# Rotation spread over the expert slots, keys stored once and doubled by their loads

## The chip, the cores and the metric

One core of a Trainium2 chip runs the whole kernel. The metric is the device time in microseconds of one launch, the median of several. The core's engines are TensorE (PE), VectorE (DVE), ScalarE (ACT) and GpSimd (POOL); SyncE (SP) only issues DMAs. DMAs issued by SyncE, ScalarE and GpSimd go to queues of their own and are carried out by 16 DMA engines.

## The reference

x is 2 x 1024 tokens of 256 columns, float32. It is normalised, and attention and a mixture of experts are added to it:

```python
xn = layernorm(x)
# attention: 16 query heads and 4 key/value heads of 16 columns; rope turns pairs of columns by position
Q, K, V = xn @ W_q, xn @ W_k, xn @ W_v
scores = rope(Q) @ rope(tile(K)).T / sqrt(16)
attn = softmax(scores) @ tile(V) @ W_o
# experts: 8, the two best of each token
topk_logits, selected = top_k(xn @ Wr, 2)
w = softmax(topk_logits)
ffn = sum over e of w_e * ((clip(silu(xn @ Wg[e]), -7, 7) * (xn @ Wu[e])) @ Wd[e])
x = x + attn + ffn
```

## The kernel before

**Head.** Tokens are taken in four blocks of 512 (k = 0 to 3, two for each batch b). For each block xn is formed, turned (xn_t) and multiplied with the router and value weights; then `queries_keys(k)` on TensorE computes three parts: m = 0 and 1 are eight query heads each (128 rows), m = 2 the keys (64 rows), all of 512 columns. ScalarE copies blocks 0 to 2 out of PSUM. On VectorE the routing chain picks the two experts of each token, counts (`rank_ps`, `total_ps` are products with one-hot rows), takes running sums by doubling steps (L785 to L790, L797 to L803) and gets each token's place in a list sorted by expert. 32 small products (`in_row` x `in_tile`, L1101) invert it, so `token_of` tells for 39 slots of 128 rows which tokens they hold.

**Expert slots.** Slot t: GpSimd gathers its rows (L509, four buffers), TensorE turns them (`to_columns`, L1160), multiplies by the gate and up weights (`gate_up`, L1167), turns the activation (`act_columns`, L1175) and multiplies it with the down weights (`down` of slot t - 2, L1184). ScalarE does SiLU (L668) and two copies out of PSUM (L671, L675); VectorE clips (L950), multiplies (L952) and copies y (L958). SyncE stores y (L384).

**Rotation.** The first 12 slots carry one part each (`PARTS`, 12 pairs of block and m). VectorE swaps neighbours (L868), the products with cosine and sine are made on GpSimd (L520, L527) or VectorE (L873), VectorE adds (L840); ScalarE rounds the sum to its high part rope_hi (L651), VectorE subtracts to get rope_low (L858), and SyncE stores both: queries to q_hl (L374, L375), keys to k_st (L378). For keys the difference of the two quarters of 256 columns is appended (L847), and each half is stored twice, since scores are products of stacked high and low parts. Three buffers are used in turn; a buffer is written again only when its stores are through (`qk_stored`).

**First maxima.** The softmax needs each query's maximum over keys before the exponentials. It is computed a unit ahead of its use: `score_first`, `score_high`, `score_low` on TensorE (L1112, L1114, L1122, L1129), `take_gain` on ScalarE (L657) and reductions on VectorE (L899 to L909). For the first two units these 32 items lie beside the last 21 slots (`SHARED`). From slot 12 on SyncE loads ka, kb and qs for groups 0 and 1.

**Attention.** Eight groups g of one key head, two units h each (half of the queries), eight key blocks kt each. `scores` puts ones x ms (minus the maximum, L1235) into PSUM and adds kb x qs (L1239); for odd kt it adds to the same bank the product with the keys' difference instead of starting again. ScalarE takes the exponential of two banks of 1024 (L702), `values` multiplies them with V (L1249). For even kt `values_between` splits `values` in two halves with score_high and score_low in between. SyncE's `period` loads, at the start of group g, kb for g + 1, ka for g + 2 and, once VectorE has turned them, the maxima ms (`load_m`, L421), then queries. In group g TensorE waits for the maxima of the second unit at kt = 7 of the first (`m_loaded[1]`, L1309).


## Time and profile before

| | us |
|---|---|
| median of three runs | 579.81 |
| lowest, highest | 579.05, 579.84 |
| profiled execution | 576.07 |
| its span | 574.3 |
| TensorE busy | 526.5 (92%) |
| VectorE busy | 396.3 (69%) |
| ScalarE busy | 383.5 (67%) |
| GpSimd busy | 173.2 (30%) |

The stages in the profiled execution: head to 61 us, expert slots to 232 us, attention to the end. A busy share is a mean over stages with different limits, so each stage is read for itself. The chain of work that ended last is 73% TensorE, 12% VectorE and 6% DMA.

### The profile page before, as it was taken

To read this page: it belongs to the slowest core of one execution; us is meant where nothing else is said; L and a number is where in the kernel's file an instruction comes from. 1 tells how busy PE (TensorE), PEld (TensorE's weight loads), DVE (VectorE), ACT (ScalarE), POOL (GpSimd) and SP (SyncE) were. 2 spreads that over 40 slices of the span, in tenths; PEclk is the share of its full clock that TensorE was granted. 3 is DMA by queue.
4 is the path that set the end of the run, shared out by engine and by line. 5 is a ranking of instruction groups with operands and counts; after the bars stand their busy time and mean duration, and the time that the engine had idled before them with its cause. 6 is when DMAs were issued, how large, how long until landed. Compare 5 with 4: busy or idle time off the path is not lost.

```text
span 574.3 us, 9921 instructions
## 1 busy us (share of the span) xinstructions
PE 526.5 (92%) x3464; PEld 249.3 (43%) x3464; DVE 396.3 (69%) x920; ACT 383.5 (67%) x548; POOL 173.2 (30%) x208
## 2 busy tenths in 40 slices
PE   1996748897999998999999999999999999999997
PEld 1832324454555554444444444444444444444433
DVE  4578756961666666587788887888888788785123
ACT  3421412431333433799999999999999999998673
POOL 3015854541222210012416422551344342600000
PEclk9997987897999999999999999999999999999999
DMA  8950235566642120310511421422224113100101
GB/s 293 375 184 1 80 133 170 169 183 193 170 138 74 59 62 29 103 38 19 131 47 45 115 58 41 102 65 75 57 58 119 31 57 84 30 2 21 46 29 55
DMA packets 39566, 53.72 MB, mean 94 GB/s; under 512 B 7936, under 2 KB 25728, under 8 KB 39520
## 3 DMA queue, kind: packets, MB, share of 16 engines
q1 hardware_dynamic: 32624, 40.25, 23.9%
q0 software_dynamic: 3408, 9.31, 5.9%
q10 hardware_dynamic: 3488, 3.55, 1.8%
q8 instruction: 28, 0.46, 0.3%
q14 instruction: 18, 0.15, 0.1%
HBM read 36.18 MB, written 16.65 MB: 92 GB/s over the span
## 4 chain that ended last, share of the span: by engine, by line
PE 73%; DVE 12%; DMA 6%; issue 3%; ACT 2%; SPq 2%; POOL 2%; DVEq 0%; ACTq 0%; POOLq 0%
PE bank L1249 21%; PE bank L1239 9%; PE bank L1112 9%; PE bank L1167 8%; PE bank L1129 7%; PE bank L1235 6%; PE bank L1184 4%; PE bank L1285 3%; DMA k_st<-rope_low 3%; PE bank L1122 2%; DMA rows_out<-xn 2%; DVE xn_t L907 2%; DVE xn L983 2%; SPq L378 1%; PE bank L1072 1%
## 5 line engine op out<-in xcount | busy, mean ns | idle before, releaser
L702 ACT ACTIVATE big<-bank 128x1024 f32<-128x1024 f32 x256 | 252.9, 1024 | 18.6 <-PE bank L1239 18.3
L1249 PE MATMUL bank<-big,v_st 128*32 128x256 f32 (+1 forms) x1472 | 148.3, 474 | 2.8 <-DVE xn L983 2.8
L1239 PE MATMUL bank<-qs,kb 64*128 64x512 f32 x512 | 120.0, 408 | 0.7 <-ACT big L702 0.7
L904 DVE TENSOR_REDUCE mx<-bank 128x1 f32<-128x512 f32 x128 | 87.8, 686 | 27.9 <-PE bank L1129 20.1
L899 DVE TENSOR_REDUCE mx<-bank 128x1 f32<-128x512 f32 x128 | 87.9, 687 | 22.1 <-PE bank L1114 20.0
L1167 PE MATMUL bank<-big,xn 128*128 x156 | 82.6, 654 | 15.9 <-ACT xn L671 15.4
L907 DVE CUSTOM_DVE_ANT_0 xn_t<-bank,xn_t 128x512 f32<-128x512 f32 x128 | 87.5, 684 | 4.5 <-PE bank L1129 1.5
L657 ACT ACTIVATE xn_t<-bank 128x512 f32<-128x512 f32 x128 | 76.7, 599 | 20.4 <-PE bank L1114 12.2
L1239 PEld LDWEIGHTS bank<-qs,kb 64*128 64x128 f32 x512 | 57.7, 185 | 19.4 <-ACT big L702 12.3
L1112 PE MATMUL bank<-ka,qs 64*128 64x512 f32 x128 | 63.4, 495 | 0.4 <-DVE mx L904 0.4
L1114 PE MATMUL bank<-ka,qs 64*128 64x512 f32 x128 | 63.3, 495 | 0.0
L509 POOL DMA_INDIRECT xn<-xn_d,token_of x39 | 39.5, 1013 | 75.8 <-PE bank L1160 67.6
L589 POOL TENSOR_TENSOR xn<-xn,rden 128x256 f32<-128x256 f32 x15 | 9.5, 636 | 170.0 <-DVE rden L987 153.3
L1129 PE MATMUL bank<-ka,qs 64*128 64x512 f32 x128 | 59.2, 462 | 0.1
L1112 PEld LDWEIGHTS bank<-ka,qs 64*128 64x128 f32 x128 | 23.4, 183 | 74.5 <-DVE mx L904 47.2
L668 ACT ACTIVATE xn<-bank 128x256 f32<-128x256 f32 x39 | 14.8, 379 | 60.0 <-PE bank L1167 59.9
L1122 PE MATMUL bank<-ka,qs 64*128 64x512 f32 x128 | 53.2, 416 | 0.0
L1235 PE MATMUL bank<-ms,ones_r 64*128 64x512 f32 x256 | 51.9, 401 | 0.0
L1249 PEld LDWEIGHTS bank<-big,v_st 128*32 128x32 f32 x1472 | 29.3, 107 | 50.0 <-issue 47.4
L950 DVE TENSOR_SCALAR xn<-xn 128x256 f32<-128x256 f32 x39 | 15.7, 402 | 49.9 <-ACT xn L668 49.9
L1184 PE MATMUL bank<-big,xn 128*128 x156 | 43.7, 406 | 5.4 <-DVE xn L958 5.4
L1167 PEld LDWEIGHTS bank<-big,xn 128*128 128x128 f32 x156 | 28.5, 200 | 46.0 <-issue 45.2
(140 smaller groups left out, 611.7 us busy)
## 6 DMA issues: line engine op xcount, KB each, us to landing
qs<-q_hl SPq DMA_DIRECT2D x64, 128.0 KB, 2.7
rows_out<-xn SPq DMA_DIRECT2D x39, 128.0 KB, 2.6
ka<-k_st SPq DMA_DIRECT2D x16, 256.0 KB
kb<-k_st SPq DMA_DIRECT2D x16, 256.0 KB
xs<-in_L_attn_x SPq DMA_DIRECT2D x4, 512.0 KB, 6.3
big<-in_L_ffn_Wg SPq DMA_DIRECT2D x16, 128.0 KB, 6.5
big<-in_L_ffn_Wu SPq DMA_DIRECT2D x16, 128.0 KB, 6.6
big<-in_L_ffn_Wd SPq DMA_DIRECT2D x16, 128.0 KB, 6.5
```

The source lines that it names most:

```text
L657: act.activation(gain[k % 2], max_bank(v, 4 * k), ACT.Relu).then_inc(gain_ready, 1)
L702: act.activation(probs[kt % 2][:, 2 * j:2 * j + 2, :].rearrange("p r q -> p (r q)"), st_ps[j][:, :], ACT.Exp, scale=1.0 / math.sqrt(HD)).t ...
L899: nc.vector.reduce_max(mx[h][:, STEPS + k, 0:1], max_bank(v, i), axis=X_AXIS).then_inc(mx_taken, 1)
L904: nc.vector.reduce_max(mx[h][:, STEPS + k, 1:2], max_bank(v, i), axis=X_AXIS).then_inc(mx_taken, 1)
L907: nc.vector.tensor_tensor_reduce(larger, max_bank(v, i + 1), gain[k % 2], scale=1.0, scalar=-FAR, op0=ALU.add, op1=ALU.max, accum_out=mx[h ...
L1112: mm(low.rearrange("p (c n) -> p c n", c=2), qs[q][0:STACK, j, rows], ka[p][0:STACK, :, QUART:HALF], start=True, stop=True).then_inc(mx_sc ...
L1129: mm(max_bank(v, i).rearrange("p (c n) -> p c n", c=2), qs[q][0:STACK, j, rows], ka[p][0:STACK, :, 0:QUART], start=True, stop=True).then_i ...
L1167: last = mm(gu_ps[i % 2][:, :], rows_t[i % 2][:, c, :], wgu[:, e, c, :], start=(c == 0), stop=(c == C - 1))
L1184: last = mm(y_ps[i % 2] if y is None else y, act_t[i % 2][:, c, :], wdn[:, e, c, :], start=(c == 0), stop=(c == C - 1))
L1235: mm(out[i], ones_r[half[i], :], ms[v][half[i], j, :], start=True, stop=False)
L1239: last = mm(out[i], kb[p][half[i], kt // QT, keys], qs[q][half[i], j, :], start=False, stop=True, skip_group_check=kt % 2 == 1)
L1249: last = mm(o_ps[32 * r:32 * (r + 1), columns], v_st[p][:, key_block(kt), :], probs[kt % 2][:, r, columns], start=(kt == 0 and columns.sta ...
```

## The change

- **Parts.** The 12 parts are ordered by batch (keys of both blocks, then queries) and lie at slots 1, 3, 5, 7, 9, 11, 14, 17, 20, 23, 26 and 29. There are four buffers in place of three. Five parts have their cosine product on VectorE. Block 3 is copied out of PSUM by ScalarE in slot 2.
- **Keys.** A key part now has 128 rows of 512 columns: the rotated keys on 64 partitions and three differences of neighbouring quarters on the other 64. It is stored once (high and low part) into k_hl. ka and kb are loaded in eight DMAs each, which read 16 rows twice (`twice`: a first dimension of 2 with no stride).
- **Scores.** Key blocks go in chains of four: only kt % 4 = 0 starts from ones x ms, the other three add differences. `values_between` is used for three of four kt, split at 128 columns.
- **Stores of y** are issued by ScalarE, all but the last two.
- **Loads.** SyncE loads ka of group 0 at slot 6, queries at 10 and 14, kb and the rest at slots 18 to 27; the first maxima lie beside the last 26 slots, and TensorE waits there for ka with a count of 128, and for the queries.
- **Routing.** The running sums are two scan instructions; in_tile's first product goes from GpSimd to VectorE; the counts are made after two parts of block 0, block 3 entirely after the inverse.

```diff
-    k_st = nc.dram_tensor("k_st", [B, KV, STACK, 2, KCOLS], F32, kind="Internal").ap()
+    k_hl = nc.dram_tensor("k_hl", [B, 2, 2, KV * HD, 2 * HALF], F32, kind="Internal").ap()
...
-        PARTS = [(k, 2) for k in range(BLOCKS - 1)] + [(k, m) for k in range(BLOCKS) for m in range(2)] + [(BLOCKS - 1, 2)]
+        PARTS = [(k, m) for b in range(B) for k, m in ((2 * b, 2), (2 * b + 1, 2), (2 * b, 0), (2 * b, 1), (2 * b + 1, 0), (2 * b + 1, 1))]
         NP = len(PARTS)
-        VECTOR_COS = (3, 5, 7)
+        VECTOR_COS = (3, 5, 7, 9, 11)
         AHEAD = 2
+
+        PART_SLOTS = (1, 3, 5, 7, 9, 11, 14, 17, 20, 23, 26, 29)
+        KEYS_LOAD, FIRST_LOAD, SECOND_LOAD = 6, 10, 14
+        LATE_LOADS = {18: (0,), 21: (1,), 24: (2, 3), 27: (4, 5)}
...
-            return kt // QT * QT + 2 * (1 - kt % 2) + kt // 2 % 2
+            return kt // QT * QT + (3, 1, 2, 0)[kt % QT]
...
-                    for j, half in enumerate((rope_hi, rope_hi, rope_lo, rope_lo)):
-                        sp.dma_start(k_st[b, :, HD * j:HD * (j + 1), k % 2, :],
-                                     half[n][0:KV * HD, :].bitcast(F32)).then_inc(done, 16)
-
-
-            def store_y(t, i):
-                sp.wait_ge(y_copied, t + 1)
-                sp.dma_start(rows_out[bass.ts(t, P), :], y_s[i]).then_inc(y_stored[i], 16)
-
-            for q in range(NP):
-                store_part(q)
-                if q >= 2:
-                    store_y(q - 2, (q - 2) % 4)
-            for t in range(NP - 2, NP):
-                store_y(t, t % 4)
+                    k_rows = [k_hl[b, k % 2, j].rearrange("d (u c) -> u d c", u=2) for j in range(2)]
+                    sp.dma_start(k_rows[0], rope_hi[n][:, :].bitcast(F32)).then_inc(done, 16)
+                    sp.dma_start(k_rows[1], rope_lo[n].bitcast(F32)).then_inc(done, 16)
...
+            def twice(g, j, half, cols):
+
+                kv = g % KV
+                return k_hl[g // KV, half, j, HD * kv:HD * (kv + 1), cols].unsqueeze(0).to_broadcast(
+                    [2, HD, cols.stop - cols.start])
+
             def load_ka(g, p):
 
-                src = k_st[g // KV, g % KV]
-                sp.dma_start(ka[p][0:STACK, :, :].bitcast(F32), src[:, :, QUART:KCOLS]).then_inc(ka_loaded[p], 16)
-                sp.dma_start(ka[p][STACK:P, :, :].bitcast(F32), src[:, :, 0:HALF]).then_inc(ka_loaded[p], 16)
+                for half in range(2):
+                    for j in range(2):
+                        low, high = 2 * HD * j, STACK + 2 * HD * j
+                        sp.dma_start(ka[p][low:low + 2 * HD, half, :].bitcast(F32),
+                                     twice(g, j, half, slice(QUART, KCOLS))).then_inc(ka_loaded[p], 16)
+                        sp.dma_start(ka[p][high:high + 2 * HD, half, :].bitcast(F32),
+                                     twice(g, j, half, slice(0, HALF))).then_inc(ka_loaded[p], 16)
 
             def load_kb(g, p):
-
-                src = k_st[g // KV, g % KV]
-                for s in range(2):
-                    sp.dma_start(kb[p][STACK * s:STACK * (s + 1), :, :].bitcast(F32),
-                                 src[:, :, QUART:KCOLS]).then_inc(kb_loaded[p], 16)
+                for half in range(2):
+                    for j in range(4):
+                        sp.dma_start(kb[p][2 * HD * j:2 * HD * (j + 1), half, :].bitcast(F32),
+                                     twice(g, j % 2, half, slice(HALF - P, 2 * HALF - P))).then_inc(kb_loaded[p], 16)
...
+            def parts_stored(last):
+                for q in range(max(0, last - NB + 1), last + 1):
+                    sp.wait_ge(qk_stored[q % NB], stored_before(q + NB))
+
+            for t in range(SLOTS):
+                q = part_at(t)
+                if q is not None:
+                    store_part(q)
+                if t == KEYS_LOAD:
+                    parts_stored(1)
+                    load_ka(0, 0)
+                if t == FIRST_LOAD:
+                    parts_stored(3)
+                    load_q(0, 0, 0)
+                if t == SECOND_LOAD:
+                    parts_stored(5)
+                    load_q(0, 1, 1)
+                for n in LATE_LOADS.get(t, ()):
+                    sp.wait_ge(rows_t_ready, t)
+                    if n == 0:
+                        load_kb(0, 0)
+                    elif n == 1:
+                        load_ka(1, 1)
+                    else:
+                        load_q(1, (n - 2) // 2, 2 + (n - 2) // 2, [n % 2])
                 if t == SLOTS - 7:
                     sp.wait_ge(m_turned_ready, 1)
                     load_m(0)
-                n = t - NP
-                if n == 0:
-                    load_ka(0, 0)
-                elif n in (1, 2, 3, 4):
-                    load_q(0, (n - 1) // 2, (n - 1) // 2, [(n - 1) % 2])
-                elif n == 5:
-                    load_ka(1, 1)
-                elif n == 6:
-                    load_kb(0, 0)
-                elif n in (7, 8, 9, 10):
-                    load_q(1, (n - 7) // 2, 2 + (n - 7) // 2, [(n - 7) % 2])
-                store_y(t, t % 4)
+            for t in range(SLOTS - 2, SLOTS):
+                sp.wait_ge(y_copied, t + 1)
+                sp.dma_start(rows_out[bass.ts(t, P), :], y_s[t % 4]).then_inc(y_stored[t % 4], 16)
+            parts_stored(NP - 1)
...
+            def store_y(t, i):
+                act.wait_ge(y_copied, t + 1)
+                act.dma_start(rows_out[bass.ts(t, P), :], y_s[i]).then_inc(y_stored[i], 16)
+
+            for t in range(SLOTS):
+                expert(t, t % 2, first=t == 0, last=t == SLOTS - 1, beside=shared_with(t))
+                if t == 0:
+                    high_part(0)
+                if t == 2:
+                    copy_projected(BLOCKS - 1)
+                if t >= 3:
+                    store_y(t - 3, (t - 3) % 4)
+                if part_at(t) is not None and part_at(t) + AHEAD - 1 < NP:
+                    high_part(part_at(t) + AHEAD - 1)
+            store_y(SLOTS - 3, (SLOTS - 3) % 4)
...
-            link(nc.vector.tensor_copy(sums[0][:, :, :].rearrange(flat), total_ps))
-            src, step = 0, 1
-            while step < 2 * NT:
-                a, z = sums[src], sums[1 - src]
-                nc.vector.tensor_copy(z[:, 0:step, :], a[:, 0:step, :])
-                link(nc.vector.tensor_tensor(z[:, step:, :], a[:, step:, :], a[:, 0:2 * NT - step, :], ALU.add))
-                src, step = 1 - src, 2 * step
-            incl = sums[src]
-
-            link(nc.vector.tensor_tensor(over[:, :, :], incl[:, 2 * NT - 1, :].unsqueeze(2).to_broadcast([P, E, NT]),
+
+            link(nc.vector.tensor_tensor_scan(sums_flat, within[:, :, :].rearrange(flat), total_ps, 0.0, ALU.mult, ALU.add))
+
+            link(nc.vector.tensor_tensor(over[:, :, :], sums[:, :, 2 * NT - 1:].to_broadcast([P, E, NT]),
                                          limit[:, :, :], ALU.is_gt))
             link(nc.vector.reduce_sum(n_tiles[:, :], over[:, :, :], axis=X_AXIS))
-            csrc, step = 1, 1
-            while step < E:
-                a, z = cum[csrc] if step > 1 else n_tiles, cum[1 - csrc]
-                nc.vector.tensor_copy(z[:, 0:step], a[:, 0:step])
-                link(nc.vector.tensor_tensor(z[:, step:], a[:, step:], a[:, 0:E - step], ALU.add))
-                csrc, step = 1 - csrc, 2 * step
-            ends = cum[csrc]
-
-            link(nc.vector.tensor_tensor(n_tiles[:, :], ends[:, :], n_tiles[:, :], ALU.subtract))
-            link(nc.vector.tensor_scalar(n_tiles[:, :], n_tiles[:, :], float(P), None, ALU.mult))
-
-            link(nc.vector.tensor_tensor(totals[:, :, :].rearrange(flat), incl[:, :, :].rearrange(flat), total_ps, ALU.subtract))
-            link(nc.vector.tensor_tensor(totals[:, :, :].rearrange(flat), totals[:, :, :].rearrange(flat),
-                                         rank_ps, ALU.add))
+            link(nc.vector.tensor_tensor_scan(ends[:, :], ones[:, 0:E], n_tiles[:, :], 0.0, ALU.mult, ALU.add))
+            link(nc.vector.tensor_scalar(starts[:, 1:], ends[:, 0:E - 1], float(P), None, ALU.mult))
...
-                        nc.vector.tensor_tensor(rope_a[n][0:rows_q, HALF:KCOLS], rope_a[n][0:rows_q, 0:QUART],
-                                                rope_a[n][0:rows_q, QUART:HALF], ALU.subtract).then_inc(rope_done, 1)
+                        nc.vector.tensor_tensor(rope_a[n][rows_q:P, 0:QUART], rope_a[n][0:rows_q, 0:QUART],
+                                                rope_a[n][0:rows_q, QUART:HALF], ALU.subtract)
+                        nc.vector.tensor_tensor(rope_a[n][rows_q:P, QUART:HALF], rope_a[n][0:rows_q, QUART:HALF],
+                                                rope_a[n][0:rows_q, P:P + QUART], ALU.subtract).then_inc(rope_done, 1)
...
-            queries_keys(0)
+            queries_keys(0, [0, 1])
 
             pe.wait_ge(choices_ready, 1)
-            hot = onehot[:, :, :, :].rearrange("p k t e -> p (k t e)")
-            mm(rank_ps, earlier[:, :], hot, start=True, stop=True)
-            mm(total_ps, ones[:, :], hot, start=True, stop=True).then_inc(counts_ready, 1)
+            hot = onehot[:, :, :, :].rearrange("p k t e -> p e (k t)")
+            mm(rank_ps.rearrange("p (e n) -> p e n", e=E), earlier[:, :], hot, start=True, stop=True)
+            mm(total_ps.rearrange("p (e n) -> p e n", e=E), ones[:, :], hot, start=True, stop=True).then_inc(counts_ready, 1)
+            queries_keys(0, [2])
...
+                    pe.wait_ge(stacks_padded, 5)
+                    pe.wait_ge(pj_copied, 3 * BLOCKS)
+                    pe.wait_ge(ka_loaded[0], 128)
...
-                first = 2 * (kt % 2) + kt // 2 % 2
+                first = (0, 2, 3, 1)[kt % QT]
                 keys = slice(first * P, (first + 1) * P)
-                if kt % 2 == 0:
+                if kt % QT == 0:
...
-                values(p, kt, s, u, slice(0, QUART))
+                values(p, kt, s, u, slice(0, P))
                 score_low(*score)
                 scores(q, kv, p, kt + 1, s + 1, 1, None, (1,))
-                values(p, kt, s, u, slice(QUART, HALF))
-
-            pe.wait_ge(kb_loaded[0], 32)
+                values(p, kt, s, u, slice(P, HALF))
...
-                        if kt % 2 == 0 and not last:
+                        if kt % QT < QT - 1 and not last:
```

On SyncE, the stores of the last query part and of a key part and the first loads, before (tensor written, tensor read, shape of the written pattern):

```order
L375 DMA q_hl<-rope_low 8x16x512
L384 DMA rows_out<-xn 128x256
L378 DMA k_st<-rope_hi 4x16x768 x2
L378 DMA k_st<-rope_low 4x16x768 x2
L384 DMA rows_out<-xn 128x256 x3
L407 DMA ka<-k_st 64x2x512
L408 DMA ka<-k_st 64x2x512
L384 DMA rows_out<-xn 128x256
L401 DMA qs<-q_hl 32x2x512 x2
```

After, the store of the second key part, one query part, and the first of the loads of ka:

```order
L388 DMA k_hl<-rope_hi 2x64x512
L389 DMA k_hl<-rope_low 2x64x512
L384 DMA q_hl<-rope_hi 8x16x512
L385 DMA q_hl<-rope_low 8x16x512
L413 DMA ka<-k_hl 32x1x512
L415 DMA ka<-k_hl 32x1x512
```

The stores of keys are two in place of four, and of another shape; the loads of ka are eight of 32 rows in place of two of 64, and stand between the stores of parts.

On SyncE at the start of attention, before: kb, ka, the maxima, queries.

```order
L414 DMA kb<-k_st 64x2x512 x2
L407 DMA ka<-k_st 64x2x512
L408 DMA ka<-k_st 64x2x512
L421 DMA ms<-m_turned 4x8x32 x4
L401 DMA qs<-q_hl 32x2x512 x4
```

After, from the last two loads of ka on (the eight of kb and the other six of ka stand ahead):

```order
L413 DMA ka<-k_hl 32x1x512
L415 DMA ka<-k_hl 32x1x512
L428 DMA ms<-m_turned 4x8x32 x4
L399 DMA qs<-q_hl 32x2x512 x4
L428 DMA ms<-m_turned 4x8x32 x4
```

The maxima keep their shape and now stand behind sixteen loads in place of four.

On TensorE in attention, an even and the beginning of an odd key block, before:

```order
L1112 MATMUL bank<-ka,qs 128x512
L1114 MATMUL bank<-ka,qs 128x512
L1239 MATMUL bank<-qs,kb 128x512 x3
L1122 MATMUL bank<-ka,qs 128x512
L1249 MATMUL bank<-big,v_st 32x256 x4
L1129 MATMUL bank<-ka,qs 128x512
L1239 MATMUL bank<-qs,kb 128x512
L1249 MATMUL bank<-big,v_st 32x256 x4
L1112 MATMUL bank<-ka,qs 128x512
L1114 MATMUL bank<-ka,qs 128x512
L1235 MATMUL bank<-ms,ones_r 128x512 x2
L1239 MATMUL bank<-qs,kb 128x512 x2
```

After, one key block of the chain and the last of it:

```order
L1126 MATMUL bank<-ka,qs 128x512
L1128 MATMUL bank<-ka,qs 128x512
L1252 MATMUL bank<-qs,kb 128x512 x3
L1136 MATMUL bank<-ka,qs 128x512
L1262 MATMUL bank<-big,v_st 32x128 x4
L1143 MATMUL bank<-ka,qs 128x512
L1252 MATMUL bank<-qs,kb 128x512
L1262 MATMUL bank<-big,v_st 32x384 x4
L1126 MATMUL bank<-ka,qs 128x512
L1128 MATMUL bank<-ka,qs 128x512
L1248 MATMUL bank<-ms,ones_r 128x512 x2
L1252 MATMUL bank<-qs,kb 128x512 x2
```

The products of L1248 (ones x ms) are there in one of four key blocks instead of one of two, and the values are cut at 128 columns.

## Rows read from the trace of the kernel before

**Rows 1.** Timeline of the head: start, duration (us), engine, line, operation [idle before <- releaser].
```profile
32.45 12.86 PE L1082 MATMUL bank<-xn_t,wqk 128*128 128x512 f32 x28
...
44.93 1.34 ACT L644 ACTIVATE rope_low<-xn,partition_no 128x1248 bf16<-128x1248 bf16 x1
...
52.64 0.70 PE L1101 MATMUL bank<-rope_low,xn 128*128 128x78 bf16 x8 [0.44 <-DVE xn L830]
...
53.14 4.72 PE L1082 MATMUL bank<-xn_t,wqk 128*128 128x512 f32 x8
...
58.61 0.41 PE L1160 MATMUL bank<-ident,xn 128*128 128x128 f32 x2 [0.76 <-DMA xn<-xn_d,token_of]
```

**Rows 2.** Timeline, ScalarE: SiLU of slots 0, 12, 13, 18 and 38.
```profile
61.60 0.38 ACT L668 ACTIVATE xn<-bank 128x256 f32<-128x256 f32 x1
...
121.24 0.39 ACT L668 ACTIVATE xn<-bank 128x256 f32<-128x256 f32 x1 [1.89 <-PE bank L1167]
...
124.26 0.39 ACT L668 ACTIVATE xn<-bank 128x256 f32<-128x256 f32 x1 [1.92 <-PE bank L1167]
...
147.10 0.39 ACT L668 ACTIVATE xn<-bank 128x256 f32<-128x256 f32 x1 [1.32 <-PE bank L1167]
...
226.32 0.38 ACT L668 ACTIVATE xn<-bank 128x256 f32<-128x256 f32 x1 [1.32 <-PE bank L1167]
```

**Rows 3.** Waits, 55 to 145 us: who waited for whom: us in total, times, longest.
```profile
ACT rope_hi L651 <- DMA k_st<-rope_low: 20.0, 3, 7.0
```

**Rows 4.** Timeline, VectorE: the sums of two parts in consecutive slots.
```profile
108.27 0.68 DVE L840 TENSOR_TENSOR rope_a<-rope_a,rope_b 128x512 f32<-128x512 f32 x1
...
112.41 0.68 DVE L840 TENSOR_TENSOR rope_a<-rope_a,rope_b 128x512 f32<-128x512 f32 x1
```

**Rows 5.** SyncE's issues of y (ns min/median/max); page: SiLU on ScalarE (busy us, mean ns).
```profile
L384 SPq DMA_DIRECT2D rows_out<-xn x39: 319/338/1957, 79.8 to 232.3; - x39
...
L668 ACT ACTIVATE xn<-bank 128x256 f32<-128x256 f32 x39 | 14.8, 379 | 60.0 <-PE bank L1167 59.9
```

**Rows 6.** DMA queue of SyncE: packets, MB, share; windows 74:78, 110:114, 276:280, 253:255.
```profile
q1 hardware_dynamic: 131, 0.38, 24.1%
...
q1 hardware_dynamic: 365, 0.56, 53.0%
...
q1 hardware_dynamic: 521, 0.96, 99.7%
...
q1 hardware_dynamic: 210, 0.33, 51.3%
```

**Rows 7.** Timeline, SyncE's queue: kb, m and q in group 2.
```profile
315.74 1.21 SPq L414 DMA_DIRECT2D kb<-k_st  x2
...
320.51 2.28 SPq L421 DMA_DIRECT2D ms<-m_turned  x4
334.61 1.72 SPq L401 DMA_DIRECT2D qs<-q_hl  x4
```

**Rows 8.** Timeline around slot 16; last, the window: busy by engine, granted clock, DMA share, GB/s.
```profile
131.40 1.88 PE L1167 MATMUL bank<-big,xn 128*128 x4
...
137.54 2.07 PE L1184 MATMUL bank<-big,xn 128*128 x4 [3.83 <-DVE xn L958]
...
139.41 3.62 PE L1167 MATMUL bank<-big,xn 128*128 x4
...
140.00:145.00 5.00, 5.00 (x14) 2.53 (x12) 1.04 (x4) 1.04 (x3) 0.87 (x1) 0.63 0.89 246
```

**Rows 9.** Chain of waits in attention: start, us, what.
```profile
306.93 0.42 PE bank L1112
...
309.39 0.43 PE bank L1112
...
309.82 0.23 PE bank L1235
...
312.01 0.42 PE bank L1112
```

More of the change, by code:

```diff
@@ L51, in build @@
     QUART = HALF // 2
+    NB = 4
     KCOLS = HALF + QUART
@@ L125, in build @@
         n_tiles = sb("n_tiles", [P, E])
-        cum = [sb(f"cum{i}", [P, E]) for i in range(2)]
+        ends = sb("ends", [P, E])
+        starts = sb("starts", [P, E])
+        slot_row = sb("slot_row", [P, SLOTS])
         slot_no = sb("slot_no", [P, SLOTS, E])
@@ L236, in build @@
         lo_ready = sem("lo_ready")
-        qk_stored = [sem(f"qk_stored{m}") for m in range(3)]
+        qk_stored = [sem(f"qk_stored{m}") for m in range(NB)]
         route = sem("route")
@@ L1238, in scores @@
                         pe.wait_ge(mx_taken, banks)
-                    last = mm(out[i], kb[p][half[i], kt // QT, keys], qs[q][half[i], j, :], start=False, stop=True, skip_group_check=kt % 2 == 1)
+                    last = mm(out[i], kb[p][half[i], kt // QT, keys], qs[q][half[i], j, :], start=False, stop=True, skip_group_check=kt % QT > 0)
                 if parts[-1] == 1:
```

183 lines of the change are left out of this document (86 added, 97 removed).

## The prediction

> **What bounds the kernel now.** I read the page first, then the chain of waits, then the timeline stage by stage. The profiled execution spans 574.3 us and took 576.07 us, 3.7 us less than the median of the runs (579.81). The sum is made against 576.07, and its change is then put on the median. There are four stages.
>
> *Head, 0 to 61 us.* The routing chain on VectorE looks like the bound, but it is not alone: TensorE runs the projections until 45.3 us (28 instructions in 12.86 us, 0.459 us each), and ScalarE, which first copies block 2 out of PSUM, makes its half of in_tile only from 44.93 to 46.27 [rows 1]. Then come the 32 products of the inverse, ended at 53.34, and slot 0's rows are there at 58.61.
>
> *The 39 expert slots.* The reader should see the start of each slot's SiLU on ScalarE [rows 2]: slot 0 at 61.60, slot 12 at 121.24, slot 38 at 226.32, 164.7 us from first to last. Undisturbed slots come 3.02 us apart. The 20 steps from slot 18 to slot 38, which also carry first maxima, take 79.2 us, or 3.96 each: 32 items on 21 slots are 1.52 a slot, so an item costs 0.94/1.52 = 0.62 us. TensorE is the bound there. In slots 0 to 17 about 30 us are lost; ScalarE waits 20.0 us there before it may write rope_hi, because the key stores haven't left the buffer [rows 3].
>
> *Attention, 232 to 523 us.* The chain is TensorE's without a gap: 2.46 us from one score_first to the next where kt is even, 2.62 where it is odd [rows 9]. ScalarE's exponentials follow closely.
>
> *Last group.* TensorE again.
>
> **The change, part by part.**
>
> *Routing.* The scans and the earlier counts take some 5 us off VectorE, and in_tile's product goes from GpSimd to VectorE. But block 2 still leaves TensorE at 32.45 + 24 x 0.459 = 43.5, since only the order of the counts and four instructions is changed, and ScalarE's part of in_tile still ends at 46.3. So the inverse starts there: 4 x 0.70 us [rows 1] give 49.1 in place of 53.34. Now all three parts of block 3 follow: 12 instructions at 0.43 to 0.59 us (8 took 4.72 us [rows 1]), to 54.3 or 56.2. That, not the gather, is late next, since the gather would land near 53.8. Slot 0 starts **3.3 us** earlier (bounds 1 and 5).
>
> *Rotation spread over slots.* The floor from slot 0 to slot 38 is 38 x 3.02 + 31 items x 0.62 = 134. With parts in every slot VectorE set a step of 4.14 us [rows 4]; with a part in every second slot it has little to do in between, so a part costs between 0 (made up for in the next slot) and 4.14 - 3.02 = 1.12 us. I take 0.6 for twelve (7.2), since GpSimd's multiplications now lie here too, and 2.3 for ScalarE's three copies of block 3 in slot 2 and for the start. Slots without any storage wait: 143.5, that is **-21.2** (bounds -28 and -11).
>
> *Stores of y from ScalarE's queue.* On SyncE's queue one issue takes 0.338 us in the median and 1.957 at worst [rows 5]. ScalarE's three activations of a slot take 0.38 us each [rows 5], so 3.02 - 1.14 = 1.9 us are free. Even the worst issue is just covered: **0**. Uncovered, it is paid in each of 37 slots.
>
> *Fewer base products.* Only every fourth key block starts from ones_r x ms. In the groups that run ahead, three of four steps become the 2.46 kind: 3 x 2.46 + 2.62 = 10.0 for 10.16. But two such steps in a row let a score wait for the exponential that frees its bank; I take -0.07 for four steps, 28 times: **-2** (bounds -4.5 and +8). In the last group a base pair costs 0.23 us [rows 9], two pairs 0.46, four times: **-1.8**.
>
> *Keys stored once, doubled by loads.* This decides. Bytes stored for a key part fall from 4 x 192 KB to 2 x 256 KB. But look at how many of the 16 DMA engines a transfer of each shape keeps busy [rows 6]. The k_st stores, written as 4x16x768, hold the queue at 24.1%: 4 of 16, although several are queued at once, so all of them use the same four. While the stores written as 8x16x512 go (with some y stores) the share is 53.0%: 8 of 16. Loads of 64x2x512 and 32x2x512 reach 99.7%. The share goes by the first dimension. The new key stores are 2x64x512, and the new key loads read a pattern whose first dimension is the doubling, 2 (the destination is 32x1x512). By the rows they run on **2 engines of 16**, the same two, one after the other.
>
> The Trainium skill says this as a rule (DMA: Bandwidth & Descriptors, section on why a DMA increments its semaphore by 16): the engine count is the largest k up to 16 that divides the slowest dimension of both patterns, and the queues of SyncE and ScalarE take the lowest-numbered k. By that rule, too, both transfers run on two engines; the rows agree at 4, at 8 and at 16, and none shows 2.
>
> Price: 131 packets of 3 KB on four engines in 4.0 us are 0.122 us each [rows 6], or 0.08 for 2 KB; 2 KB packets of the q loads take 0.513 x 2.0 x 16/210 = 0.078; those of the key loads now 0.997 x 4.0 x 16/521 = 0.122. I take 0.083, as with two engines little else goes to the same memory; the ends are 0.078 and 0.122. One key part is 256 packets on two engines, 10.6 us; one ka or kb load the same.
>
> (a) *Slots.* Key parts stored from about 64.5 and 71.5 leave at 88. SyncE waits for that at slot 6 before it loads ka, and holds back the store of part 3 behind it. In order on the two engines: part 2 to 91, ka to 101.6, part 3 to 104.4, part 4 to 107, q for slot 13 to 109.5. TensorE is at slot 13 near 98.6: **+10.9**. Then TensorE comes back at the lower clock: after a wait of 3.83 us in slot 16, the wide products took 3.62 us for the usual 1.88, and the narrow ones ahead of them 2.07, twice their usual time too; the clock granted in the stretch is 0.63 on the mean, thus the lower level of 1.2 GHz for much of it [rows 8]. Together +2.8.
>
> (b) *Attention.* At the start of a group SyncE issues kb, then ka, then the maxima m. In group 2 kb is issued at 315.74, m at 320.51, and the scores before the point where TensorE needs m are ready at 334.61 [rows 7]: 19.2 us after kb, with 0.3 for that step. Now kb and ka are 2 x 10.6 on the two engines, behind them m, whose pattern (4x8x32) uses these engines as well: an estimated 1.3 us from issue to the first byte, 21.2, and 1.5 for m (the page gives the smaller q loads 2.7 from issue to landing in all), together 24.0. TensorE waits 4.8 us, and returns cold, 2.8: 7.6 us in each of the six groups 0 to 5 that load both (group 6 loads kb alone, 10.6, in time): **+46**.
>
> Sum: -3.3 - 21.2 + 10.9 + 2.8 - 2 + 46 - 1.8 = +31.4. On 576.07: 607.5; on the median **611**.
>
> **The rivals.**
> *Full width.* The doubled loads go over all engines, as the loads from k_st do now. Then neither (a) nor (b) is there: 579.81 - 28.3 = **551.5**, faster. For it: no row shows a source with a repeated dimension. Against it: every row goes by the first dimension. Its own range is 543 to 566.
> *Two engines, but m is not held up,* for instance because its few packets pass the others or the packets are shorter than 0.067 us: only (a) remains, 551.5 + 13.7 = **565**. The row of 0.078 speaks against it.
> *Slow packets.* The loads keep 0.122 us on two engines: kb and ka take 31.2 us, each of six groups waits 14.8 + 2.8: 611 + 60 = **671**. For it: that is what these bytes take today. Against: today 16 engines write to 64 partitions together.
> *ScalarE's queue.* An issue of y of over 2.5 us passes the 1.9 free; at 2.7 it costs 0.8 x 37 = 30, alone enough to bring full width back to 581; no row reaches that.
>
> **How the numbers follow.** Forecast 0.76, slow packets 0.04, full width 0.15, m not held up 0.03, ScalarE's queue 0.02. The wait of a group may be 3.5 us (0.078 and a warm clock later) to 10, so the forecast's own range is 574 to 645; the end below is taken to 564 to include the case where m passes. A measurement can tell 0.2% from no change: faster 0.19, same 0.01, slower 0.80.
>
> **What would show it.** In the trace of the changed kernel: the queue's share near 12% while keys are stored or loaded; a wait of TensorE at slot 13 for q of some 11 us; in groups 0 to 5 a wait at the step before the second unit, 3 to 10 us, with the clock low after it; group 6 without one. The slots else 3.0 to 3.7 us apart, slot 0's SiLU near 58.3, ScalarE's issues below 1 us. I am wrong if the share is near 100% in the key loads: then it is 551.

## The result and the profile after

The changed kernel takes 628.9 us in the median of four runs (626.3 to 629.8) where the kernel before takes 579.7: a ratio of 1.084 (95% interval 1.081 to 1.088), 8.4% slower. The prediction was 611 in a range of 564 to 645. The profiled execution spans 626.5 us, before 574.3.

I read the page first. From its fourth part, the chain that ended last, and its fifth (busy us, mean ns of one | idle before it, and what ended most of it):

```profile
span 626.5 us, 10198 instructions
...
PE 58%; SPq 17%; DMA 16%; DVE 4%; ACT 3%; issue 2%; DVEq 0%; ACTq 0%
PE bank L1262 13%; DMA ms<-m_turned 9%; PE bank L1181 9%; PE bank L1252 8%; SPq L415 6%; PE bank L1126 5%; PE bank L1198 4%; SPq L413 4%; PE bank L1143 4%; SPq L421 4%; PE bank L1096 4%; DMA k_hl<-rope_low 3%; PE bank L1248 3%; PE bank L1298 3%; SPq L428 2%
...
L1126 PE MATMUL bank<-ka,qs 64*128 64x512 f32 x128 | 63.6, 497 | 13.6 <-DMA qs<-q_hl 13.4
...
L1248 PE MATMUL bank<-ms,ones_r 64*128 64x512 f32 x128 | 29.6, 459 | 41.6 <-DMA ms<-m_turned 41.6
```

A third of the chain is now SyncE's queue and DMA. L421, L413 and L415 are the issues of kb and ka, L428 that of m. TensorE stands still 13.4 us once for q and 41.6 us for m.

The waits between 240 and 640 us, then two of those between 50 and 240 us (who waited for whom: us in total, times, longest):

```profile
PE bank L1248 <- DMA ms<-m_turned: 41.6, 6, 8.1
```

```profile
PE bank L1126 <- DMA qs<-q_hl: 13.4, 1, 13.4
...
ACT rope_hi L675 <- DMA k_hl<-rope_low: 4.8, 1, 4.8
```

Six waits, one in each group that loads kb and ka, 6.9 us on the mean. The last row answers to [rows 3]: one store wait of 4.8 us where there were three of 20.0 in all.

What happens at the start of a group (SyncE's queue in the timeline; group 1), and the same place in the chain of waits (start, us, what):

```profile
278.90 5.01 SPq L421 DMA_DIRECT2D kb<-k_hl  x8
283.96 0.62 SPq L413 DMA_DIRECT2D ka<-k_hl  x1
...
291.95 2.46 SPq L415 DMA_DIRECT2D ka<-k_hl  x1
294.45 3.09 SPq L428 DMA_DIRECT2D ms<-m_turned  x4
298.32 1.72 SPq L399 DMA_DIRECT2D qs<-q_hl  x4
```

```profile
296.94 9.31 DMA ms<-m_turned
...
306.29 0.79 PE bank L1248 x2
```

From the first issue of kb to the m that TensorE needs, 27.4 us pass, and 9.3 of them come after the last issue of m; before, m was issued 4.8 us after kb [rows 7]. The issues themselves are held: the same instruction (L415) takes 0.575 us at least and 2.46 here.

SyncE's DMA queue while keys are loaded (packets, MB, share of 16 engines), from 286 to 294 us:

```profile
q1 hardware_dynamic: 178, 0.34, 11.8%
```

Two of 16 engines are 12.5%. The 178 packets in 8 us are 0.090 us for one packet on each of two engines. With [rows 6] this makes a row of its own at two engines, beside those at 4, 8 and 16. (The prediction names 32x2x512 with the 99.7%; that window has loads of 64x2x512 and m only, and the window with q loads shows 51.3%.)

The slots, by the SiLU on ScalarE, as [rows 2] (slots 0, 10, 12, 13 and 38):

```profile
61.65 0.38 ACT L691 ACTIVATE xn<-bank 128x256 f32<-128x256 f32 x1 [0.85 <-PE bank L1181]
...
100.35 0.36 ACT L691 ACTIVATE xn<-bank 128x256 f32<-128x256 f32 x1
...
108.51 0.36 ACT L691 ACTIVATE xn<-bank 128x256 f32<-128x256 f32 x1
127.04 0.38 ACT L691 ACTIVATE xn<-bank 128x256 f32<-128x256 f32 x1 [3.15 <-PE bank L1181]
...
222.68 0.38 ACT L691 ACTIVATE xn<-bank 128x256 f32<-128x256 f32 x1 [1.32 <-PE bank L1181]
```

Slot 0 starts no earlier than before. Slot 12 is reached 12.7 us earlier, then 18.5 us pass to slot 13. From slot 0 to 38 it is 161.0 us, before 164.7. From slot 38's SiLU to the end it is 403.8 us, before 574.3 - 226.3 = 348.0. So of the 52.2 us that the span grew, the head has 0.1, the slots -3.7 and all that follows +55.8.

### The profile page after: what moved, and what is told of

Same layout as the page of the kernel before. It is cut to its first block, busy times and chain, and to the rows that moved or that the text cites. A ratio compares the mean times of both kernels' runs of the same rounds, so it can differ in the third digit from the quotient of the medians.

```text
span 626.5 us, 10198 instructions
## 1 busy us (share of the span) xinstructions
PE 535.2 (85%) x3560; PEld 250.7 (40%) x3560; DVE 390.7 (62%) x907; ACT 385.4 (62%) x551; POOL 169.7 (27%) x212
## 4 chain that ended last, share of the span: by engine, by line
PE 58%; SPq 17%; DMA 16%; DVE 4%; ACT 3%; issue 2%; DVEq 0%; ACTq 0%
PE bank L1262 13%; DMA ms<-m_turned 9%; PE bank L1181 9%; PE bank L1252 8%; SPq L415 6%; PE bank L1126 5%; PE bank L1198 4%; SPq L413 4%; PE bank L1143 4%; SPq L421 4%; PE bank L1096 4%; DMA k_hl<-rope_low 3%; PE bank L1248 3%; PE bank L1298 3%; SPq L428 2%
## 5 line engine op out<-in xcount | busy, mean ns | idle before, releaser
L1262 PE MATMUL bank<-big,v_st 128*32 128x128 f32 (+2 forms) x1696 | 157.2, 443 | 1.7 <-DVE xn L997 1.5
L1252 PE MATMUL bank<-qs,kb 64*128 64x512 f32 x512 | 136.6, 432 | 6.1 <-ACT big L732 5.9
L917 DVE TENSOR_REDUCE mx<-bank 128x1 f32<-128x512 f32 x128 | 87.5, 683 | 67.1 <-PE bank L1136 58.3
L1181 PE MATMUL bank<-big,xn 128*128 x156 | 81.2, 645 | 5.9 <-ACT xn L694 5.4
L1252 PEld LDWEIGHTS bank<-qs,kb 64*128 64x128 f32 x512 | 64.4, 191 | 37.1 <-ACT big L732 31.3
L1126 PE MATMUL bank<-ka,qs 64*128 64x512 f32 x128 | 63.6, 497 | 13.6 <-DMA qs<-q_hl 13.4
L1248 PE MATMUL bank<-ms,ones_r 64*128 64x512 f32 x128 | 29.6, 459 | 41.6 <-DMA ms<-m_turned 41.6
L1128 PE MATMUL bank<-ka,qs 64*128 64x512 f32 x128 | 63.7, 498 | 0.0
L1143 PE MATMUL bank<-ka,qs 64*128 64x512 f32 x128 | 62.4, 488 | 0.0
L1136 PE MATMUL bank<-ka,qs 64*128 64x512 f32 x128 | 57.8, 451 | 0.0
L1262 PEld LDWEIGHTS bank<-big,v_st 128*32 128x32 f32 x1696 | 34.0, 108 | 58.8 <-issue 52.6
L963 DVE TENSOR_SCALAR xn<-xn 128x256 f32<-128x256 f32 x39 | 17.3, 443 | 41.9 <-ACT xn L691 41.9
L596 POOL TENSOR_SCALAR rope_a<-rope_a,gate 128x256 f32<-128x256 f32 x32 | 29.3, 921 | 51.2 <-DMA rope_a<-rows_out,place_i 51.2
L1198 PE MATMUL bank<-big,xn 128*128 x156 | 41.4, 389 | 1.6 <-DVE xn L971 1.6
```

What stands on the lines that cost most here:

```text
L917: nc.vector.reduce_max(mx[h][:, STEPS + k, 1:2], max_bank(v, i), axis=X_AXIS).then_inc(mx_taken, 1)
L1126: mm(low.rearrange("p (c n) -> p c n", c=2), qs[q][0:STACK, j, rows], ka[p][0:STACK, :, QUART:HALF], start=True, stop=True).then_inc(mx_sc ...
L1128: mm(high.rearrange("p (c n) -> p c n", c=2), qs[q][STACK:P, j, rows], ka[p][STACK:P, :, 0:QUART], start=True, stop=True).then_inc(mx_scor ...
L1143: mm(max_bank(v, i).rearrange("p (c n) -> p c n", c=2), qs[q][0:STACK, j, rows], ka[p][0:STACK, :, 0:QUART], start=True, stop=True).then_i ...
L1181: last = mm(gu_ps[i % 2][:, :], rows_t[i % 2][:, c, :], wgu[:, e, c, :], start=(c == 0), stop=(c == C - 1))
L1198: last = mm(y_ps[i % 2] if y is None else y, act_t[i % 2][:, c, :], wdn[:, e, c, :], start=(c == 0), stop=(c == C - 1))
```

## The experiments

Theory: a copy whose slowest dimension is 2 keeps two DMA engines busy, and what is queued behind it on these engines, m above all, comes late. Rivals: the loads are late for their number or their bytes; narrow stores and not loads are the cause; the transfers disturb each other wherever they stand in the queue. All spans below are those of the profiled executions, and the edits are shown shortened.

**The key loads alone at full width.** Number of DMAs and bytes as in the change, but each copies 16 rows of both halves:

```
- ka[p][low:low + 2 * HD, half, :]  <- twice(g, j, half, slice(QUART, KCOLS))     # 2 x 16 x 512
+ ka[p][low:low + HD, :, :]         <- once(g, j, slice(QUART, KCOLS))            # 16 x 2 x 512
```

> The changed kernel, with each key load (ka, kb) as a copy of 16 rows by the two halves of the keys into 16 partitions instead of one half of 16 rows written twice: the same 16 DMAs and the same 1 MB a group, but no copy whose slowest dimension is 2. Theory (the loads use two DMA engines and the load of m stands behind them): the six waits of L1248 for ms, 6.9 us each, and the 2.1 us or so of cold clock behind each go, since a group took 50.3 us where it took 41.3: 6 x 9 = 54 us less; the wait for q at slot 13 (13.4 us) falls to between 0 and 9, as the keys' stores stay narrow. 628.9 - 54 - 8 = 567 (558 to 580). Rival (the loads are slow for their number, their bytes or because DRAM is read twice, not for their width): the waits stay and the time stays above 615.

Measured: 570.8 us (569.3 to 572.5), ratio to the kernel before 0.990 (0.984 to 0.996). No wait for m is left. While kb and ka are loaded, the queue now shows (263 to 267 us):

```profile
q1 hardware_dynamic: 459, 0.65, 57.9%
```

and in that group SyncE issues each ka DMA in 0.42 us, none held. The wait for q at slot 13 is 7.7 us. So 58 us hang on the shape of 16 copies a group, with number and bytes unchanged.

**Loads and stores at full width.** Beside the above, a key part is stored in four DMAs of 64 rows:

```
- sp.dma_start(k_rows[j], part[n])                                     # 2 x 64 x 512, j = 0, 1
+ for u in range(2): sp.dma_start(k_hl[b, k % 2, j, :, cols_u], part[n][rows_u, :])   # 64 x 512
```

> As loads_full, and the two stores of a key part as four of 64 rows, each with one long run of 2 KB a row, so that no copy of keys at all has a slowest dimension of 2. Theory: beside what loads_full gives, ScalarE's high part in slot 10 no longer waits for a store (4.8 us) and the q load of slot 13 is issued in time, so 3 to 13 us under loads_full: 558 (550 to 566), which is 3 to 5% under the kernel before; the 551.5 of the prediction's rival at full width if the head had gained its 3.3 us. Rival (stores were not what held the slots): equal to loads_full within 2 us.

Measured: 561.0 us (558.8 to 564.2), ratio 0.971 (0.966 to 0.977). ScalarE waits for no store, the wait for q is 2.6 us, and slots 0 to 38 take 145.3 us. The slots did what was forecast. But the whole is 9.5 us above the 551.5 of the prediction's rival: the loss is in attention, where from slot 38 on this kernel takes 355.3 us and the kernel before 348.0.

**The stores alone at full width.** The edit of the stores, with the narrow loads kept.

> The changed kernel with its narrow loads, and the key stores alone in four DMAs of 64 rows. Theory: the groups' waits stay (6 x 9 us); in the slots ScalarE's wait of 4.8 us for a key store at slot 10 goes, and the q load of slot 13, issued 8 to 15 us sooner, still has the narrow ka load ahead of it on the same engines: 628.9 - 5 - 3 = 621 (612 to 626). Rival (the narrow stores are what fills the queue in the slots and the loads only follow): the wait for q under 3 us, 610 to 614.

Measured: 617.8 us (614.9 to 618.8), ratio 1.070 (1.065 to 1.076). TensorE still waits for m (same columns as above):

```profile
PE bank L1249 <- DMA ms<-m_turned: 46.0, 6, 8.5
```

and 8.4 us for q. The time is in the range. The slots (151.8 us) gained 9.2, and what follows them stayed (404.3 us for 403.8). The narrow stores cost about 10 us, the narrow loads about 57.

**m issued ahead of the keys.** All transfers as in the change, only SyncE's order in a group differs:

```
+ for h in range(2):  wait m_turned_ready; load_m(1 - h)
+     if h == 0:      load_kb(g + 1, 1 - p); load_ka(g + 2, p)
-   (kb and ka ahead of both)
```

> The changed kernel with its narrow loads, and one difference of order: in each group SyncE issues the first load of m ahead of kb and ka, which otherwise stay as they are. Theory (m waits in the queue behind the narrow loads): the six waits and the cold clock behind them go, 54 us less: 575 (565 to 590), if the second m, the q and the key loads, now later by the time of one m, still land before they are read. Rival (m lands late since narrow loads slow every transfer beside them, or because the engines are shared): still waits of 3 us and more, over 600.

Measured: 576.1 us (573.5 to 578.3, ten runs), ratio 0.998 (0.995 to 1.001). No wait of TensorE for m is left, with the very same narrow loads. What costs 53 us is thus not that the keys are slow, but what stands behind them.

**The narrow loads alone, in the kernel before.**

```
- sp.dma_start(ka[p][0:STACK, :, :], src[:, :, QUART:KCOLS])             # 64 x 2 x 512
+ four of: ka[p][low:low + 2 * HD, half, :] <- k_st[..., 2 * HD * j:2 * HD * j + HD, half, cols], twice   # 2 x 16 x 512
```

> The kernel before, whose stores and stored keys stay as they are, with its ka and kb loads alone in the form of the change: 16 rows read from the first of the two stored copies and written twice, 16 DMAs a group on a slowest dimension of 2, in place of four DMAs on a slowest dimension of 64. Theory: the loads alone bring the groups' waits, 6 x 7 to 9 us: 579.7 + 42 to 54 = 622 to 634, perhaps 1 to 5 more in the slots. Rival (the waits come from the whole: stores from another queue, keys read while they are stored, SyncE's order in the slots): under 595.

Measured: 656.6 us (654.9 to 657.2), ratio 1.139 (1.133 to 1.145):

```profile
PE bank L1243 <- DMA ms<-m_turned: 47.6, 6, 8.6
```

This is 23 us over the upper end of what I expected. The six waits for m are 7.9 us each; with what follows them, the part from slot 38 on takes 57.4 us more than in the kernel before (405.4 for 348.0), 9.6 a group where I had at most 9. The slots I had put at 1 to 5 us, and they took 183.6 us for 164.7. Two waits make up most of it, from 50 to 250 us:

```profile
PE bank L1120 <- DMA qs<-q_hl: 12.8, 1, 12.8
DVE xn L966 <- DMA rows_out<-xn: 11.3, 2, 7.0
```

TensorE waits 12.8 us at slot 18 for q, whose load SyncE issues behind that of ka. VectorE waits 7.0 us near slot 26 for a y store; SyncE issued y stores behind ka and kb there, and the kernel before waits for y once, 5.5 us. That the queue shared with y is the cause of the second wait is likely; I didn't test it alone. The loads by themselves make this kernel slower than the whole change does.

**Why attention loses: chains of two again.** both_full with the scores chained in pairs, as before.

```
- first = (0, 2, 3, 1)[kt % QT];   if kt % QT == 0: base products
+ first = 2 * (kt % 2) + kt // 2 % 2;   if kt % 2 == 0: base products
```

The order of the key blocks, kb's columns, `values_between` for even kt only and the split of the values at 256 columns are also as before.

> both_full with one part of the change undone: the scores of a step are again chained in pairs (the first of two key blocks starts from m, the second adds to it) instead of in fours, with kb's columns and the split of the values as in the kernel before. In the traces a half group takes 21.4 to 22.0 us in both_full where it took 20.64 in the kernel before, and PE waits for the exponentials 8.4 us in all, where the kernel before waits for none; the last group takes 40.97 against 42.67. Theory (the saved m products only let PE run ahead of ScalarE, whose exponentials and gain take 2.57 us a step either way, and the wait then costs ScalarE a pause; in the last group, where PE has more beside it than ScalarE, they do save): 13 half groups x 0.8 less 1.7 = 8.7 us faster than both_full's 561.0: 552.3 (549 to 556), and half groups of 20.6. Rival (what both_full loses in attention comes from elsewhere, the 16 small key loads among it, and fours save 2 + 1.8 as forecast): 562 to 566.

Measured: 553.6 us (551.5 to 554.4), ratio 0.958 (0.955 to 0.962), both_full 0.971 against the kernel before in its own session. One half group, from transposition to transposition on VectorE, in the kernel before, in fours and in pairs:

```profile
317.38 0.71 DVE L983 STREAM_TRANSPOSE xn<-bank 128x512 f32<-128x512 f32 x1
...
338.02 0.71 DVE L983 STREAM_TRANSPOSE xn<-bank 128x512 f32<-128x512 f32 x1
```

```profile
321.03 0.71 DVE L996 STREAM_TRANSPOSE xn<-bank 128x512 f32<-128x512 f32 x1
...
342.68 0.71 DVE L996 STREAM_TRANSPOSE xn<-bank 128x512 f32<-128x512 f32 x1
```

```profile
317.06 0.71 DVE L996 STREAM_TRANSPOSE xn<-bank 128x512 f32<-128x512 f32 x1
...
337.65 0.71 DVE L996 STREAM_TRANSPOSE xn<-bank 128x512 f32<-128x512 f32 x1
```

20.64, 21.65 and 20.59 us. How a chain of four loses it, in TensorE's timeline of both_full, and in ScalarE's:

```profile
326.06 0.50 PE L1127 MATMUL bank<-ka,qs 64*128 64x512 f32 x1
326.39 0.40 PE L1251 MATMUL bank<-qs,kb 64*128 64x512 f32 x2
327.63 0.49 PE L1251 MATMUL bank<-qs,kb 64*128 64x512 f32 x1 [0.84 <-ACT big L731]
```

```profile
324.49 1.02 ACT L731 ACTIVATE big<-bank 128x1024 f32<-128x1024 f32 x1
...
326.55 1.02 ACT L731 ACTIVATE big<-bank 128x1024 f32<-128x1024 f32 x1 [1.04 <-PE bank L1251]
```

TensorE's L1251 needs the bank that the exponential begun at 326.55 is still reading; that exponential had itself waited 1.04 us for TensorE. The two banks of scores are all there is between the two engines. With short steps in a row each engine stops for the other, and ScalarE can't make up a pause, for its two exponentials and its gain fill the step:

```profile
249.34 1.94 ACT L731 ACTIVATE big<-bank 128x1024 f32<-128x1024 f32 x2
251.41 0.60 ACT L679 ACTIVATE xn_t<-bank 128x512 f32<-128x512 f32 x1
```

That is 2.54 us of a step of 20.64/8 = 2.58. This is read from the order of the waits: no run had a third bank, and none took the base products, the place of the values and their split apart. ScalarE's waits for L1251 between 230 and 500 us, in fours and in pairs:

```profile
ACT big L731 <- PE bank L1251: 11.0, 13, 1.1
```

```profile
ACT big L731 <- PE bank L1251: 3.5, 13, 0.3
```

In the last group, where ScalarE has less to do (no gains), fours are better: its two half groups take 22.72 + 18.25 = 41.0 us in fours, 23.66 + 19.03 = 42.7 in pairs.

**y stores back on SyncE's queue.** In full_pairs:

```
- act.dma_start(rows_out[...], y_s[i])      # ScalarE, slot t stores y of slot t - 3
+ sp.dma_start(rows_out[...], y_s[i])       # SyncE, the same slot
```

> full_pairs with the y stores of the slots issued again by SyncE, each at the same slot as ScalarE issued it, behind that slot's part store and loads. Theory (as forecast, the move to ScalarE's queue costs and gives nothing by itself): equal to full_pairs within 1.5 us. Rival 1 (0.5 us of ScalarE a slot was on the path): 3 to 10 us faster. Rival 2 (a y store behind SyncE's waits for key and query stores holds its buffer until DVE needs it): 3 to 15 us slower, with DVE waiting for rows_out in slots 6 to 16.

Measured: 553.3 us (553.2 to 555.9), full_pairs 553.6 on the same chip. No difference, as forecast.

**All rotation parts in slots 1 to 12.** In full_pairs:

```
- PART_SLOTS = (1, 3, 5, 7, 9, 11, 14, 17, 20, 23, 26, 29)
+ PART_SLOTS = tuple(range(1, 13))
```

> full_pairs with one part of the change undone: the twelve rotation parts sit in slots 1 to 12 in a row, not spread over slots 1 to 29. Theory (a slot with a part costs 0.6 us more wherever it sits, except where parts in a row make DVE or a buffer's store the bound, as the 8 us steps of slots 3 to 5 of the kernel before): 5 to 15 us slower than full_pairs, 557 to 567, in steps of 4.5 to 8 us at slots 3 to 13. Rival (spreading gives nothing, the 19 us of the slots came from the stores' number and the later shared scores): equal to full_pairs within 2 us.

Measured: 571.6 us (569.3 to 572.4), 18.0 more than full_pairs and 3 beyond the largest difference that I expected. The stretch of 62 to 105 us, dense and then spread (length, then busy us of PE, PEld, DVE, ACT and POOL, granted clock, DMA share, GB/s):

```profile
62.00:105.00 43.00, 31.81 (x102) 17.10 (x103) 40.33 (x69) 14.18 (x38) 31.67 (x25) 0.92 0.57 162
```

```profile
62.00:105.00 43.00, 38.56 (x140) 21.96 (x140) 34.81 (x70) 17.25 (x46) 25.62 (x23) 0.96 0.54 150
```

With a part in every slot VectorE is busy 94% of the time and TensorE 74%; spread, it is 81% and 90%. The wait for q is 7.2 us in dense for 2.9 in spread, another part of the 18. After slot 13 the spread kernel does six parts more and still takes only 0.6 us more to slot 38 (95.0 against 94.4).

**Fours in the last group alone.** What the two half-group times suggest:

```
+ def in_fours(g): return g == G - 1      # base products, key order and kb's columns by group
```

> full_pairs, with the chain of four kept for the last group alone (its kb columns, order of key blocks and m products as in the change), since half groups took 20.6 us in pairs against 21.6 in fours, but the last group 42.69 in pairs against 40.97 in fours. Theory (PE is late against ScalarE only in the last group): 553.6 - 1.7 = 551.9 (550.5 to 553.5), with half groups of 20.6 and a last group of 41.0. Rival (fours in the last group gain only as the groups before it run in fours too): the last group 42 to 42.7, equal to full_pairs.

Measured: 552.1 us (548.8 to 553.9). Half groups of 20.6, the last group 22.72 + 18.28 = 41.0. The group times are as expected; the 1.5 us against full_pairs is within the scatter of the medians (against the kernel before both have a ratio of 0.958), so the gain rests on the traces.

**q of slot 13 asked for two slots sooner.**

```
- KEYS_LOAD, FIRST_LOAD, SECOND_LOAD = 6, 10, 14
+ KEYS_LOAD, FIRST_LOAD, SECOND_LOAD = 6, 8, 14
```

> full_last_fours, with the first q load at slot 8 of SyncE's order instead of slot 10. In full_pairs PE waits 2.9 us for it in slot 13; it is issued behind the store of part 4, which stands in the queue until DVE's low part of slot 9 is there. Theory: issued some 5 us sooner, it lands before slot 13, the wait goes: 2.9 us faster than full_last_fours, 549 (547.5 to 551). Rival (at slot 8 it waits there for part 3's stores and holds part 4's store, and the late store holds a rotation buffer): equal to full_last_fours or up to 4 us slower.

Measured: 547.1 us (545.9 to 548.8), ratio 0.951 (0.948 to 0.953). Slots 0 and 38:

```profile
61.47 0.38 ACT L696 ACTIVATE xn<-bank 128x256 f32<-128x256 f32 x1 [0.85 <-PE bank L1186]
...
202.52 0.39 ACT L696 ACTIVATE xn<-bank 128x256 f32<-128x256 f32 x1 [1.32 <-PE bank L1186]
```

The wait is gone and the slots take 141.1 us, 4.0 less than in full_last_fours, where the wait was 2.4. The median falls by 5.0 us, 0.4 past the end of the range. This kernel is 4.9% faster than the kernel before and 12% faster than the change (0.951 against 1.084), of which it keeps the spread, the scans, the four buffers and keys stored once.

## Why the prediction was right, and where its terms were off

**Two engines.** Shown. The queue's share is 11.8%, and the shape alone, at equal bytes and number, moves 58 us. The Trainium skill's rule (DMA: Bandwidth & Descriptors, section on why a DMA increments its semaphore by 16) gives two engines for a slowest dimension of 2, and the 11.8% agrees with it. The narrow stores of keys repeat nothing and have a share of 9.7% (under Slots below), so the width is enough without the repetition.

**m behind the keys,** forecast 4.8 + 2.8 in each of six groups, 46 in all. Shown as a mechanism: with m ahead, the wait is gone. The wait was mis-sized: 6.9 us. A packet took 0.090 us, not 0.083, which makes 23.0 us of the 21.2. In group 1 27.4 us passed from kb to m in place of 24.0, and TensorE stood at the wait 20.6 us after kb in place of 19.2: 3.4 more less 1.4 makes the wait 2.0 longer there, 6.8 us. What the other 1.6 of the 3.4 us are is open; the held issues of ka are a candidate, as m was issued only 15.6 us after kb. What the lower clock costs was 2.8 in the sum. before_narrow, where nothing else differs from the kernel before in attention, has half groups with a wait of 30.5 us for 20.6 without, and a wait of 7.9: 2.0 for the clock. The windows of group 1 in the changed kernel show it (same columns as above; the two stretches are the wait and the return):

```profile
299.00:306.00 7.00, 0.47 (x6) 0.16 (x2) 0.69 (x1) 1.06 (x2) 0.00 (x0) 0.79 0.39 104
306.00:308.00 2.00, 1.71 (x8) 1.43 (x10) 0.00 (x0) 0.39 (x1) 0.00 (x0) 0.50 0.02 7
```

After 7 us of near rest the granted clock is 0.50, the lower level of 1.2 GHz, and the first L1248 takes 0.79 us for two. So six groups cost 6 x (6.9 + 2.0) = 53.4 for 45.6.

**Fewer base products,** forecast -2 and -1.8. The second is right: 42.7 - 41.0 = 1.7. The first has the wrong sign. Thirteen half groups took 21.4 us on the mean in loads_full and 20.6 in full_pairs: +10 us (+8 against the 20.7 of the kernel before). The step that failed is "I take -0.07 for four steps". I priced TensorE's steps alone and wrote that ScalarE follows closely, but ScalarE was level with the step, and what TensorE saved was no gain but, by the reading above, a swing that two banks could not take up. The prediction named this and had a bound of +8, and then took the value from TensorE's steps alone. In the changed kernel itself it shows less: after slot 38 there are 55.8 us, less 53.4 for the waits and plus 1.7 for the last group, so about 4, since a wait for m also lets ScalarE catch up.

**Slots.** Without any wait the slots take 141.1 us (full_last_fours_q8), forecast 143.5. A part costs less than the 0.6 taken: (141.1 - 134 - 2.9)/12 = 0.35, with 2.9 for slot 2, whose step is 5.87 us. That spreading is what does it was shown by full_pairs_dense. The waits were forecast at 10.9 + 2.8. The change needs 161.0 us where full_last_fours_q8 needs 141.1, 19.9 more. Of these 13.4 are the wait for q, 2.5 more than forecast. The step that holds it is otherwise 18.5 - 13.4 = 5.1 us for 3.0, and the next one 4.6 for 4.1: about 2.7 for the lower clock, as forecast. The last 4 us are in the steps from slot 1 to slot 12 (64.8 to 108.5, against 64.6 to 104.2), and I had not charged them: ScalarE waits 4.8 us at slot 10 for a key store.

That 13.4 lies so near 10.9 is in part luck, since both ends of the wait came over 10 us late. By the forecast TensorE is at slot 13 near 98.6 and q lands at 109.5. In the chain of waits, and in TensorE's timeline:

```profile
78.33 21.41 DMA k_hl<-rope_low
```

```profile
122.50 0.76 PE L1126 MATMUL bank<-ka,qs 64*128 64x512 f32 x1 [13.38 <-DMA qs<-q_hl]
```

TensorE was there at 109.1 and q at 122.4. The key stores were mis-sized. They were issued at 70.8 and 77.8 for the 64.5 and 71.5 of the forecast, and left at 99.7 for 88. SyncE's queue from 80 to 84 us, when it holds nothing but them:

```profile
q1 hardware_dynamic: 68, 0.14, 9.7%
```

That is a share for two engines again, at 4.0 x 2/68 = 0.118 us for a packet where I took 0.083. TensorE's own 10.5 us are 3.3 of the head, 4 of the steps just named and 3 by which 98.6 was too early in any case: without a wait, full_last_fours_q8 needs 43.2 us from slot 0's SiLU to that product, for 40.3 in the forecast.

**Head,** forecast -3.3 (slot 0 at 58.3). Measured 61.65, no gain, and the routing is not the reason. In two windows of 18 to 20 us, before and after (columns as above), the same products run at different speeds:

```profile
18.00:20.00 2.00, 2.00 (x21) 2.00 (x20) 1.39 (x6) 1.62 (x4) 0.00 (x0) 1.00 1.09 381
```

```profile
18.00:20.00 2.00, 2.00 (x12) 2.00 (x12) 1.51 (x6) 1.25 (x3) 0.00 (x0) 1.00 1.09 382
```

21 matmuls in 2 us against 12. In the profiled execution of the change TensorE ran slowly for longer at the start, and began the projections at 30.5 us where it was 26.0. loads_full, whose head is the change's, ran it as the kernel before did (projections from 26.1) and has slot 0 at 58.89: -2.7. In loads_full ScalarE's part of in_tile ends at 47.5, 1.2 later than forecast, and TensorE waits for it, as forecast:

```profile
46.18 1.34 ACT L666 ACTIVATE rope_low<-xn,partition_no 128x1248 bf16<-128x1248 bf16 x1
47.57 1.66 PE L1113 MATMUL bank<-rope_low,xn 128*128 128x78 bf16 x32 [2.88 <-ACT rope_low L666]
49.03 6.91 PE L1094 MATMUL bank<-xn_t,wqk 128*128 128x512 f32 x12
```

**ScalarE's queue,** forecast 0. ScalarE's issues in the changed kernel (ns min/median/max, first and last start):

```profile
L707 ACTq DMA_DIRECT2D rows_out<-xn x37: 326/326/338, 75.3 to 226.1; - x37
```

None comes near 1.9 us, and in full_pairs_y_sync moving the stores back moves nothing.

**The sum.** In spans: forecast +31.4, measured +52.2. The 20.8 between them are 7.8 in the six groups, about 6 in the fours, 3.8 in the slots and 3.4 in the head. All four go the same way, so the time lies within the range by the range's width and not by a balance of the terms. The two engines carried the sign, and without them the change is 3% faster, as the rival at full width had it in kind (551.5 forecast, 561.0 measured with the fours, 553.6 without).

## What to carry to other kernels

Look at the slowest dimension of both patterns of a DMA before anything else of it: here the same bytes in the same number of copies cost 58 us more at 2 than at 16. Ask next what stands in the queue behind a long transfer, since it was the small urgent load of m, and not the keys, that came late. And before work is taken off one engine in a pipeline of two, look whether the other is level with the step time: here it was, the saving was nothing, and the uneven steps cost more than was saved; where the balance differs (the last group here), decide it for that stretch alone.

## What was not expected of the hardware

- The time of an issue on SyncE's queue depends on what is under way. With the same 16 DMAs a group, the issues of ka took 0.42 us in the median and 1.7 at worst in loads_full, and in the changed kernel 0.65 (L413) and 1.22 (L415) in the median and 3.78 at worst. SyncE issues in order, so m's issue is put off with them. An issue of kb took 0.58 us in the median and 6.6 at worst. The worst lie in the slots behind a narrow store of keys: loads_full, which keeps the narrow stores, has 6.65 too, and stores_full, which keeps the narrow loads, has 0.68 at most. The row of the changed kernel (ns min/median/max):

```profile
L421 SPq DMA_DIRECT2D kb<-k_hl x64: 575/576/6600, 149.3 to 539.4; - x64
```

- The time at which TensorE leaves its slow start differs from one execution to the next with the same instructions: the first weight loads of 128x128 took 333 ns and later ones 190, with the change at about 18 us in the kernel before, loads_full, stores_full and full_pairs_dense, at about 22 us in m_first, before_narrow and full_pairs, and at 26 us or later in the changed kernel, both_full, full_last_fours and full_last_fours_q8, while the granted clock of 18 to 20 us is given as 1.00 in both windows above. Slot 0 then starts between 58.7 and 61.9 us among kernels with the same head, so one profile doesn't tell a gain of 3 us in the head from none.
